# The tail of a one-core transformer kernel in a new order: top-k rounds doubled up, routing rows in runs of 28 tokens

## The reference, cut to what matters

```python
x = x + _L1_conv_ref(_ln_c(x), ...)      # positions by a 3x3 conv, 4 corners x 9 taps gathered, weighed, projected
t = _to_tokens(x)
t = t + _L1_ffn_ref(_ln_t(t), ...)
# in _L1_ffn_ref:
weights = (jnp.einsum('bsd,do->bso', x, wr) + br)[..., 0]
_, idx = jax.lax.top_k(weights, k)       # k = 1568, the first 1567 are used
h = jax.nn.gelu(jnp.einsum('bkd,dh->bkh', sel, w1) + b1)
y = (jnp.einsum('bkh,hd->bkd', h, w2) + b2) * w_sel[..., None]
return jnp.zeros_like(x).at[batch_idx, sel_idx].set(y) + x
```

## Time and profile before

| | |
|---|---|
| median of the runs | 4095.86 us (3 runs, 4093.54 to 4108.44) |
| the profiled execution | 4094.89 us, span 4093.1 us |
| busy: TensorE, VectorE, ScalarE, GpSimd | 3505.1, 3083.8, 2405.6, 1995.9 us |
| image 7's experts end | about 3582 us |
| first gather of image 7 | 3648.1 us |
| last sample of image 7 added | 4032.8 us |

### The profile page before, as it was taken

One profiled execution on the slowest core, in us unless ns is written; L12 is line 12 of the kernel. 1 busy time (PEld: TensorE's weight loads), 2 busy tenths in 40 slices (PEclk: granted clock), 3 DMA queues, 4 the chain that ended last, 5 costly groups with the idle time before them and its releaser, 6 DMA issues.

```text
span 4093.1 us, 58290 instructions
## 1 busy us (share of the span) xinstructions
PE 3505.1 (86%) x21688; PEld 1885.2 (46%) x21688; DVE 3083.8 (75%) x4894; ACT 2405.6 (59%) x4152; POOL 1995.9 (49%) x1805
## 2 busy tenths in 40 slices
PE   5979997999899999999899999999899999945431
PEld 2434444454545445454545455544545455524321
DVE  6466577987699688977798678978798678855775
ACT  5746774577656776577656775577556765522110
POOL 0000064664456364655466464646466465657760
PEclk8989997999799999999899989999899989956555
DMA  4000122232222332231222332232222322235355
GB/s 114 1 8 1 40 75 70 78 100 60 72 79 86 77 96 62 79 100 57 78 80 78 81 94 63 82 88 68 77 79 75 81 83 71 86 102 134 89 126 109
DMA packets 374810, 314.91 MB, mean 77 GB/s; under 512 B 312672, under 2 KB 317024, under 8 KB 374528
## 3 DMA queue, kind: packets, MB, share of 16 engines
q0 software_dynamic: 85248, 231.33, 18.8%
q1 hardware_dynamic: 289280, 79.88, 9.1%
HBM read 279.30 MB, written 57.69 MB: 82 GB/s over the span
## 4 chain that ended last, share of the span: by engine, by line
PE 65%; DVE 12%; ACT 8%; DVEq 4%; issue 4%; POOL 3%; DMA 2%; SPq 1%; ACTq 0%
PE PS L1551 59%; PE PS L1755 3%; POOL G L452 3%; DVEq L492 2%; PE PS L1587 2%; DVE G L490 2%; DVE work L918 2%; DVE G L496 1%; ACT work L1371 1%; DVE small L904 1%; ACT small L1416 1%; DVE st L458 1%; DMA out<-xin 1%; PE PS L1591 1%; ACT xn_hl L1289 1%
## 5 line engine op out<-in xcount | busy, mean ns | idle before, releaser
L452 POOL DMA_INDIRECT G<-corner_table,index x1800 | 1995.4, 1109 | 1962.6 <-DVE index L708 674.7
L1371 ACT ACTIVATE work<-PS 128x768 f32<-128x768 f32 (+2 forms) x800 | 651.7, 823 | 279.1 <-PE PS L1551 225.6
L1443 ACT ACTIVATE work<-PS,descale 128x512 f32<-128x512 f32 (+2 forms) x896 | 566.9, 633 | 417.2 <-PE PS L1551 404.2
L818 DVE TENSOR_TENSOR work<-work 128x768 f32<-128x768 f32 (+2 forms) x496 | 480.2, 972 | 297.2 <-PE PS L1551 245.5
L918 DVE SCALAR_TENSOR_TENSOR work<-PS,descale,work 128x512 f32<-128x512 f32 (+2 forms) x896 | 603.2, 679 | 132.6 <-ACT work L1443 124.2
L1551 PE MATMUL PS<-work,xm 128*64 128x400 f32 (+3 forms) x3200 | 622.9, 502 | 0.0
L490 DVE TENSOR_TENSOR G<-G,corner_w 128x768 f32<-128x768 f32 x600 | 561.8, 952 | 64.5 <-DMA G<-corner_table,index 63.1
L1551 PE MATMUL PS<-xn_hl,xn_hh 128*128 128x384 f16 (+2 forms) x1600 | 543.9, 340 | 48.1 <-ACT work L1371 39.6
L1551 PE MATMUL PS<-xn_hl,xn_ll 128*128 128x384 f16 (+2 forms) x1600 | 539.4, 338 | 0.0
L1551 PE MATMUL PS<-work,w3s 128*64 128x384 f32 (+2 forms) x1792 | 435.9, 565 | 4.4 <-DVE small L904 4.4
L1449 ACT ACTIVATE small<-PS 128x512 f32<-128x512 f32 (+2 forms) x448 | 243.2, 543 | 237.8 <-PE PS L1551 237.1
(11 more groups left out here) (262 smaller groups left out, 4927.1 us busy)
## 6 DMA issues: line engine op xcount, KB each, us to landing
G<-corner_table,index POOLq DMA_INDIRECT x1800
corner_table<-rows_scratch SPq DMA_DIRECT2D x32, 784.0 KB
corner_table<-G SPq DMA_DIRECT2D x8, 841.0 KB, 8.5
xin<-x SPq DMA_DIRECT2D x8, 768.0 KB, 5.6
rows_scratch<-xln SPq DMA_DIRECT2D x8, 768.0 KB
x_scratch<-xB SPq DMA_DIRECT2D x8, 768.0 KB
yw_scratch<-yw SPq DMA_DIRECT2D x7, 784.0 KB, 6.6
x<-x_scratch SPq DMA_DIRECT2D x4, 784.0 KB, 6.5
```

Source lines behind the costliest of these rows:

```text
L452: GP.indirect_dma_start(G[0:rows, n % 2, tap * 4 * C:(tap + 1) * 4 * C], None, tables[b % 2], bass.IndirectOffsetOnAxis(ap=index[0:rows, c ...
L818: V.tensor_tensor(sq[0:rows, u % 4, :, 0:n], relu[0:rows, u % 2, :, 0:n], relu[0:rows, u % 2, :, 0:n], ALU.mult).then_inc(s["sq_dve"], 1)
L1371: A.activation(relu[0:rows, u % 2, :, 0:n], PS[u % 2][0:rows, :, 0:n], ACT.Relu).then_inc(s["relu_done"], 1)
L1443: A.activation(silu[:, e % 2, 0:w], S[e % 2][:, 0:w], ACT.Silu, scale=descale[:, MOE1:MOE1 + 1]).then_inc(s["silu_done"], 1)
```

## The change

1. **Tail's prologue in an order of its own.** The mixer's order and its interleaving are gone. ScalarE copies for the table first, with late tile 0's evacuations between, and casts then. Transposes go through the four S banks, the second offsets group through Y0. VectorE weighs late tiles 1 to 3 ahead of the positions.
2. **Routing rows.** For images 0 to 6 partition p holds tokens 28p to 28p + 27: a load, a store and yw have one run of 7168 bytes per partition. The FFN's matmuls read xf (channels on partitions, tokens along it) with a step of 28 elements, as the moving operand of `ffn_up` and `tail_ffn` and as the stationary one of the routing products. The tie order follows. Image 7 keeps the old order.
3. **Counts inside the sample**, between stages 1 and 2; a second round of a tile comes behind the sample. Rounds at tiles 8, 9, 9, 10, 11, 11, 12, 13, 13, 14, 15; choose_end at 15; finals at 16 to 22, one a tile.
4. **A third pair of buffers** for the finals, in the experts' weights, and loads two images ahead.
5. **Image 7 alone:** routing products and choose_start ahead of the down products; comparison and step of a round in one instruction; final and store in two halves.

```diff
-LAST_FINAL = (20, 20, 21, 22, 22, 23, 24)
+LAST_FINAL = (16, 17, 18, 19, 20, 21, 22)
+LAST_ROUNDS = (8, 9, 9, 10, 11, 11, 12, 13, 13, 14, 15)
...
+        dead = w12[:, :].bitcast(f32)
+        fin_x = (routed(x1_flat), routed(xin_flat), routed(dead))
...
         def route_dram(t, k):
+            if k < LAST:
+                return t[bass.ds(k, 1), :, :].rearrange("a (p t) c -> p (a t) c", p=RP)
             return t[bass.ds(k, 1), :, :].rearrange("a (t p) c -> p (a t) c", p=RP)
+        def routed_tokens(f):
+            return xf[:, :].rearrange("k (p t) -> k t p", p=RP) if f < LAST else xf[:, :].rearrange("k (t p) -> k t p", p=RP)
...
+            load_back(1)
             for k in range(B - 1):
-                if k + 1 < B - 1:
-                    load_back(k + 1)
+                if k + 2 < B - 1:
+                    load_back(k + 2)
...
+            for half in range(2):
+                sp.wait_ge(s["fin_ready"], B + half)
+                r = slice(half * RT // 2, (half + 1) * RT // 2)
+                sp.dma_start(route_dram(o, LAST)[:, r, :], fin_x[q][:, r, :]).then_inc(s[f"out_stored{q}"], 16)
# VectorE, prologue
+            ln_invert("g", LAST, 0)
+            for q in range(4):
+                ln_scale("g", xln, 0, q)
+            late_weigh(1, range(3))
+            for q in range(4):
+                split_l("g", LAST, 0, q)
+            late_weigh(1, range(3, 5))
+            sample_add(PREV, late_tile(0))
+            late_weigh(2)
+            sample_add(PREV, late_tile(1))
+            late_weigh(3)
+            for g in range(2):
+                positions_floor(LAST, g)
+                for step in range(4):
+                    positions_part(g, step)
+                sample_add(PREV, late_tile(2 + g))
+                if g == 1:
+                    late_weigh(4)
+                corners_index(g)
+                corners_mask(g)
...
# VectorE, a round of image 7
+                    V.scalar_tensor_tensor(got7[:, 0:NTRY], ps[:, 0:NTRY], kth[:, 0:1], incs[:, i, :], ALU.is_ge, ALU.mult)
# VectorE, image 7 alone
-            tail_out(LAST, NCH - 1)
+            dve.wait_ge(s["route_done"], 1)
+            tail_route(LAST, NCH - 1, S[1])
             dve.drain()
             choose_start(B - 1, 1, ROUNDS + 2)
+            tail_out(LAST, NCH - 1)
...
# ScalarE, prologue
+            for q in range(4):
+                act.wait_ge(s["g_scaled"], 4 * LAST + q + 1)
+                geo_table(q)
+                if q < 3:
+                    late_evac(0, (q,))
+            for q in range(4):
+                cast_h("g", LAST, 0, q)
+            for c in range(NCH):
+                geo_evac(LAST, c)
+            late_evac(1, (0, 1))
+            offsets_cm(LAST, 0)
+            offsets_tm(LAST, 0)
+            late_evac(1, (2,))
+            offsets_cm(LAST, 1)
+            offsets_tm(LAST, 1)
# TensorE, prologue
+            late_sample(0, range(4))
+            for c in range(NCH):
+                geo_transpose(LAST, c)
+            offsets(LAST, 0, range(0, 5))
+            late_sample(1, (0,))
+            offsets(LAST, 0, range(5, TAPS))
+            late_sample(1, (1,))
+            offsets(LAST, 1, range(0, 4))
+            offsets_transpose(LAST, 0)
+            late_sample(1, (2,))
+            offsets(LAST, 1, range(4, TAPS))
+            late_sample(1, (3,))
+            offsets_transpose(LAST, 1)
# TensorE, FFN
-                    src = xf[:, c * CW:(c + 1) * CW]
+                    src = routed_tokens(f)[:, c * CT:(c + 1) * CT, :]
...
-                    ins = mm(D1[0:RP, 448 + 2 * t:450 + 2 * t], xf[:, t * RP:(t + 1) * RP], wr2[:, :])
+                    ins = mm(D1[0:RP, 448 + 2 * t:450 + 2 * t], routed_tokens(f)[:, t, :], wr2[:, :])
# TensorE, tail loop
             for t in range(T):
-                for n in range(4):
-                    sample(LAST, t, n)
+                sample(LAST, t, 0)
+                sample(LAST, t, 1)
+                if t == 7:
+                    count(1, B - 1)
+                for i in rounds_of(t)[0:1]:
+                    count(i + 2, NTRY * (B - 1))
+                sample(LAST, t, 2)
```

More of the change, by code:

```diff
@@ L94, in metaformer_kernel @@
         w_mix = sb("w_mix", [C, C])
[L95 to L98, removed]
+        w12 = sb("w12", [128, 4 * E * HID], f16)
+        w1h, w1l, w2h, w2l = (w12[:, i * E * HID:(i + 1) * E * HID] for i in range(4))
         w3s = sb("w3s", [HID, E, C])
@@ L1046, in _, with late_weigh @@
                 image(k)
[L1047 to L1054, removed]
+            def late_weigh(j, pieces=range(5)):
+                for piece in pieces:
+                    weigh(PREV, late_tile(j), piece)
+            ln_invert("g", LAST, 0)
[18 more added lines that the diff above has]
+                corners_mask(g)
+                corners_weights(g, 0)
+                corners_weights(g, 1)
+            sample_add(PREV, late_tile(4))
             def views(b0, nb):
@@ L1181, in tail_norm, with tail_route @@
                 V.scalar_tensor_tensor(x3[:, r, :], tmp[:, r, :], 1.0 / XS, x3[:, r, :], ALU.mult, ALU.add).then_inc(s["skip_added"], 1)
+            def tail_route(f, c, bank):
+                r = slice(c * CT, (c + 1) * CT)
+                red(w_all[:, f, r], bank[0:RP, CT * C:CT * C + 2 * CT].rearrange("p (t two) -> p t two", two=2))
+                dve.drain()
+                V.tensor_scalar(w_all[:, f, r], w_all[:, f, r], descale[0:RP, ROUTE:ROUTE + 1], brc[:, 0:1], ALU.mult, ALU.add)
             def tail_out(f, c):
@@ L1188, in tail_out @@
                 dve.wait_ge(s["tdown_done"], n + 1)
-                red(w_all[:, f, r], bank[0:RP, CT * C:CT * C + 2 * CT].rearrange("p (t two) -> p t two", two=2))
-                dve.drain()
-                V.tensor_scalar(w_all[:, f, r], w_all[:, f, r], descale[0:RP, ROUTE:ROUTE + 1], brc[:, 0:1], ALU.mult, ALU.add)
+                if n < 2 * NCH - 1:
+                    tail_route(f, c, bank)
                 V.tensor_tensor(yw[:, r, :], bank[0:RP, 0:CT * C].rearrange("p (t c) -> p t c", c=C), bc(fb2r[:, :], 1, CT),
@@ L1251, in _ @@
             choose_end(B - 1, 1, ROUNDS + 2)
-            dve.wait_ge(s[f"x3_back{LAST % 2}"], 16 * (LAST // 2 + 1))
-            final(LAST, fin_x[LAST % 2], yw)
+            dve.wait_ge(s[f"x3_back{LAST % NFIN}"], 16 * (LAST // NFIN + 1))
+            for half in range(2):
+                r = slice(half * RT // 2, (half + 1) * RT // 2)
+                final(LAST, fin_x[LAST % NFIN][:, r, :], yw[:, r, :], r)
         @block.scalar
@@ L1623, in offsets @@
                     pe.wait_ge(s["g_cm"], (i + 1) * NCH)
-                if g == 1 and taps[0] == 0:
+                if g == 1 and taps[0] == 0 and i < LAST:
                     pe.wait_ge(s["om_taken"], i * 2 + 1)
@@ L1887, in ties, with late_sample @@
                 mm(S[1][0:RP, 0:nb * RT], ones16[:, :], eq16[:, 0:nb * RT]).then_inc(s["tie_done"], 1)
[L1889 to L1894 removed]
+            def late_sample(j, stages):
+                for stage in stages:
+                    sample(PREV, late_tile(j), stage)
+            late_sample(0, range(4))
[11 more added lines that the diff above has]
+            offsets_transpose(LAST, 1)
+            for j in range(2, NLATE):
+                late_sample(j, range(4))
             def tail_ffn(f, c):
@@ L1940, in _ @@
             tail_last(NCH - 1)
-            count(ROUNDS + 3, 1)
             with pe.Fori(0, ROUNDS) as i:
```

132 lines of the change are left out of this document (71 added, 61 removed).

## The result

| | before | after |
|---|---|---|
| median of the runs, us | 4094.7 (4091.66 to 4108.44) | 4225.19 (4223.37 to 4226.1) |
| ratio, 95% interval | | 1.0302, 1.0285 to 1.0319 |
| profiled span, us | 4093.1 | 4223.4 |

The change makes the kernel 3.0% slower; 4058 was predicted. From the page after: TensorE's busy share and its granted clock, each in 40 slices, then the DMA queue's packets. The last fence is the clock's line of the page before.

The account below looks back on a forecast made before the run. The prediction saw a sequence of waits, no engine full. From 4094.9 it took 14.4 (prologue), 18.2 (tile 8 to last add), 1.0, 2.7 and 1.7 (last image): 4056.9, given as 4058 us; range 4036 to 4100.

Parts of the forecast that it names:

- I take nothing: TensorE's strided reads of xf in the six images ahead of the tail: cost zero, bounds nothing and 121 us.
- Rival B: Each strided xf column on TensorE costs 1.7 to 1.84 ns: 105 to 121 us, about 4170, slower; chance 0.12.
- The seventh image's FFN lies in tiles 3 to 6, where the gathers set the pace: Tail, tiles 0 to 8: pace stays the gathers', 13.1 us a tile, so no cost from that FFN's strided reads.
- Rival A: Strided xf columns on TensorE at half the upper rate, 0.83 ns each: 26 us, so 4084; chance 0.22.
- The prologue: Start of the tail: earlier table copies and index bring the first gather to 3633.7 from 3648.1, -14.4 us.
- Rival D: The prologue's chain stays as long, index no earlier than 3645: 4070; chance 0.07.
- Tiles 8 to 16: Tail with eleven rounds and choose_end: VectorE sets the pace, 136.2 us in place of 119.8.
- Tiles 16 to 24: Tail with finals on three buffers: load waits go, gathers set 98.2 us plus 4 for slowing, in place of 134.1.
- term of 4 us for slowed gathers: Allowance in tiles 16 to 24 for gathers slowed beside the finals' loads and stores: 4 us.
- rival C: Transfers and gathers collide from tile 16, finals wait as now, 20 us stay: 4078; chance 0.14.
- The last image: Image 7 alone at the end: earlier first round -1.0, eleven shorter rounds -2.7, final in halves -1.7 us.
- the likeliest case's own range: Whole kernel, spread of the forecast case with chance 0.45: 4045 to 4072 us.

Follow-up runs that it names:

- e1: The changed kernel with the old order of routing rows for all eight images, xf read contiguously; 4075.35 us, ratio 0.9934 to the kernel before.
- e4: e1 with the moving reads of xf at steps of 1, 2, 4, 7, 14, 28 elements in images 0 to 5 (wrong tokens); 4142.23 us.
- e3: The changed kernel with ScalarE writing xf in the new order, strided writes in even images, runs of 16 in odd; 4113.54 us, ratio 1.0015.
- e5: e1 with the routing products' stationary reads of xf at steps of 1 to 28 elements by image (wrong tokens); 4081.57 us.
- e12: e1 with e7's schedule of rounds and finals, old rows and 256-byte rows in memory; 4059.8 us, ratio 0.989 to the kernel before.
- e9: e6 with the finals' loads of images 3 to 6 and all seven stores cut to one row in 28; 4079.99 us beside 4098.04.
- e10: e6 with VectorE's work of the seven finals cut to one row in 28, transfers whole; 4063.43 us beside 4098.04.
- e7: e6 with rounds one a tile (8 to 18) and finals at tiles 19, 19, 20, 21, 22, 23, 24; 4062.42 us, ratio 0.99 to the kernel before.
- e6: The changed kernel with ScalarE writing xf in the new order in runs of 16, all seven images, TensorE reading contiguously; 4077.86 us, ratio 0.9941.

## Why the prediction was wrong

**The step that failed** is "I take nothing", for the strided reads of xf (bounds 0 and +121). They cost 146.5 us ahead of the tail and 11.4 in it (e1's ratio gives both back: 4068 us, 4067 expected). I chose between the bounds by VectorE's reads at a step of 8 bytes, nearer in kind. But two such elements still share a 16-byte line, while at 56 bytes none do, so that row could not speak for this case; the one at 16 bytes could. The rule of the Trainium skill that I set beside the sum (SBUF — State Buffer, Door 1: The DMA port swizzle: full rate needs two hits in a line) pointed the right way, and the trace of e4 disagrees with it in size: at two hits (step 4) TensorE is already at half its rate.

**Rival B was the mechanism**, its column price of 1.7 to 1.84 ns right (1.71), its total short. That the price fitted is partly luck: it came from a write by VectorE, and ScalarE's write at a long step costs 5.0 ns an element (e3). By B's own sum with the measured pitches: 104 x (0.765 - 0.19) + 64 x (0.765 - 0.375) + 168 x (0.216 - 0.053) = 112 us. The timeline has 98.1 us for the strided products, 71.2 and 26.9. The sum is larger because it charges all 28 products of xf an image, and the first four cost nothing: in image 3's gate TensorE idles 1.4 us behind them, waiting for ScalarE, where it idled 3.0 before.

What was left out is the clock. Before, it rises within the rest of the FFN; with reads at step 7 and above it stays at the lower level to the end (e4), and work that is not strided pays too. Sixteen down products take 3.19 us in the FFN after and 1.69 in e4's at the upper level, and the 96 an image cost 44.0 us for the six images. Where a run has both levels, the price of a strided read is the same (step 4 in e4, the loads in e5), so I put the clock's share at these 44.0; products of xf at step 28 were never granted the upper level, and so much of this split is not shown. Together that makes 142 of 146.5; where the last 4.5 lie was not traced.

**"The seventh image's FFN lies in tiles 3 to 6, where the gathers set the pace"** failed with it: 11.4 us. At 0.765 us a product TensorE sets the pace of tiles 5 to 7.

**Rival A** is out with the pitch: half the upper rate would be 0.375 us a product.

**The prologue** was right: 14.7 us less to tile 0, 14.4 forecast; the first gather is 17.0 earlier against the reduction, and ScalarE's last copy for the table ends 7.4 earlier, 7.3 forecast. Rival D is out.

**Tiles 8 to 16** were right, 135.1 for 136.2. The rows behind it were VectorE's own durations, and they carried over.

**Tiles 16 to 24**: 113.4 for 102.2. That the finals' waits for loads would go was right (none is left after; the third buffer does it, e12). The term of 4 us for slowed gathers was mis-sized: they cost 15, and not through transfers, as the prediction and rival C had it, but through VectorE's finals (e9, e10). Without these the stretch takes 96.0, near the 98.2 of the gathers alone.

**The last image** came out, 10.2 and 55.2 us for 9.9 and 55.1, but by terms that offset each other: the eleven rounds won 1.8 us in place of 2.7 (a round takes 2.54, not 2.45), the earlier first round 1.5 in place of 1.0, and the final and store in halves 2.0 in place of 1.7.

Without the failed step the forecast would stand beside e1: 4068 us (0.9934 of 4094.7) for 4058, inside the likeliest case's own range of 4045 to 4072.

The crowding of eleven rounds into eight tiles, which the prediction priced correctly, was itself a loss: e7, with one a tile and the finals later, is some 15 us faster than e6. Tiles 8 to 24 took 253.9 us before, 248.5 after, 230.5 in e7.

## What to carry to other kernels

Before a layout is changed for DMA's sake, list every engine that reads the tile and count how many 16-byte lines its read touches per element: a step that is free for one engine at 8 bytes says nothing of 56 on another, and where TensorE is last in a stage its price falls on the end in full, the clock's with it. If the order must change, make it where an evacuation passes anyway, reading PSUM at a step and writing SBUF in runs. A second bottleneck (here GpSimd's gather calls) can be slowed by long two-operand VectorE work beside it. Moving that work to where the calls have slack would be the next thing to try; no run here does only that.

## What the runs showed of the hardware

- TensorE pays 1.71 to 1.77 ns for each 16-byte line of a moving operand in f16, so 0.44 ns a column at step 2, 0.87 at 4, 1.54 at 7, 1.71 to 1.77 from 14 on (e4); a stationary load of 112 columns takes 0.216 us at step 28 (6.05 / 28) and 0.056 at step 1 (1.56 / 28, e5). Neither price changed with the clock: 0.39 to 0.40 us a product at step 4, granted 0.50 or 1.00, and 6.05 us for 28 loads at step 28 granted 0.50, 6.08 granted 0.82 in the mean.
- An FFN full of such products at steps of 7 elements and more was granted 0.50 to its end, although TensorE was busy in 42.1 of 43 us of it. At steps 1, 2 and 4 the clock rose to 1.00 within it.
- ScalarE's f16 write at a step of 224 bytes took 2.22 us for 448 elements; its read of PSUM at a step of 112 bytes with runs of 16 written took 0.54, the same as contiguous.
- GpSimd's indirect DMA calls took 2.6 us beside VectorE's two-operand f32 instructions of 2.02 us each, 4.4 at the longest, and 0.95 alone. Traffic made no such difference: 63 calls took 86.5 us at 184 GB/s (e6) and 90.2 at 73 (e9).
